# Three of four batches of x are turned by the host instead of TensorE, in an attention and mixture layer on one core

## The reference

```
x = x + layernorm(attention(layernorm(x)))
x = x + layernorm(ffn(layernorm(x)))
```

## Time and profile before

| | us |
|---|---|
| median of 3 runs | 1018.43 (1017.51 to 1020.02) |
| profiled execution | 1016.17 |
| its span, first to last instruction | 1014.4 |
| projection stage, within the span | about 0 to 297 |
| attention of the 32 groups | about 297 to 600 |
| output projection and ffn | about 600 to 1014 |

### The profile page before, as it was taken

The page is one execution under the profiler, slowest core; times in us unless marked ns, Lnnn a source line. Parts: engine busy times, 40 slices in busy tenths (PEclk is TensorE's granted clock), DMA queues, the critical chain, the costliest instruction groups (busy, mean ns, idle before and its releaser), DMA issues.

```text
span 1014.4 us, 17409 instructions
## 1 busy us (share of the span) xinstructions
PE 990.1 (98%) x6400; PEld 814.0 (80%) x6400; DVE 660.6 (65%) x1954; ACT 400.2 (39%) x682; POOL 455.2 (45%) x490
## 2 busy tenths in 40 slices
PE   6999999999999999999999999999999999999996
PEld 5888888898886666666666678999999999999996
DVE  7752443434558988998989666666666666666655
ACT  7331221210127777777777662222222222222211
POOL 1453542433439999999998911111111111111110
PEclk9999999999999999999999999999999999999998
DMA  9342442237247876765555463222222222222101
GB/s 354 151 146 84 146 145 84 83 116 195 99 148 197 217 197 173 186 163 151 140 140 145 138 209 99 86 83 84 83 83 84 84 84 83 83 79 77 54 22 41
DMA packets 78644, 127.23 MB, mean 125 GB/s; under 512 B 7776, under 2 KB 46944, under 8 KB 75488
## 3 DMA queue, kind: packets, MB, share of 16 engines
q1 hardware_dynamic: 78560, 126.13, 41.0%
HBM read 85.20 MB, written 40.37 MB: 124 GB/s over the span
## 4 chain that ended last, share of the span: by engine, by line
PE 92%; DVE 3%; DMA 2%; ACT 1%; POOL 1%; issue 1%; SPq 0%; POOLq 0%; DVEq 0%; ACTq 0%
PE bank L1287 21%; PE bank L1289 21%; PE bank L1288 21%; PE bank L1359 8%; PE bank L1381 7%; PE bank L1397 7%; DMA q_t<-shift_l 2%; PE bank L1421 2%; PE bank L1296 1%; PE bank L1547 1%; PE bank L1424 1%; PE bank L1427 1%; DVE wf_l L1195 1%; DVE bank L1018 1%; PE bank L1460 0%
## 5 line engine op out<-in xcount | busy, mean ns | idle before, releaser
L1018 DVE CUSTOM_DVE_ANT_0 bank<-bank,row_mask 128x384 f32<-128x384 f32 (+3 forms) x512 | 235.7, 517 | 49.9 <-PE bank L1359 49.8
L653 POOL TENSOR_TENSOR ln_rs<-ln_ve,minus_half 128x1 f32<-128x1 f32 x64 | 61.6, 962 | 392.6 <-DVE ln_mm L962 392.6
L837 ACT ACTIVATE prob<-bank 128x512 f32<-128x512 f32 x320 | 173.9, 599 | 34.8 <-PE bank L1381 34.5
L1287 PE MATMUL bank<-wf_h,xt_h 128*128 128x384 f32 (+1 forms) x384 | 129.7, 338 | 0.9 <-DVE z L1176 0.9
L1289 PE MATMUL bank<-wf_l,xt_h 128*128 128x384 f32 (+1 forms) x384 | 130.2, 339 | 0.0
L1288 PE MATMUL bank<-wf_h,xt_l 128*128 128x384 f32 (+1 forms) x384 | 129.6, 338 | 0.0
L1359 PE MATMUL bank<-k_t,q_t 96*128 96x384 f32 (+3 forms) x512 | 123.4, 337 | 0.4 <-DVE row_top L1018 0.3
L1287 PE MATMUL bank<-xt_h,wq_h 128*128 128x512 f32 x304 | 119.8, 394 | 0.0
L1289 PE MATMUL bank<-xt_l,wq_h 128*128 128x512 f32 x304 | 118.6, 390 | 0.0
L1288 PE MATMUL bank<-xt_h,wq_l 128*128 128x512 f32 x304 | 118.5, 390 | 0.0
L711 POOL TENSOR_TENSOR key_sum<-key_sum,prob 128x512 f32<-128x512 f32 x93 | 117.8, 1293 | 0.0
(11 more groups left out here) (118 smaller groups left out, 1882.4 us busy)
## 6 DMA issues: line engine op xcount, KB each, us to landing
q_t<-q_scratch SPq DMA_DIRECT2D x32, 512.0 KB, 5.5
q_scratch<-turn_h SPq DMA_DIRECT2D x16, 512.0 KB, 2.7
q_scratch<-turn SPq DMA_DIRECT2D x16, 512.0 KB, 3.0
q_t<-q_scratch SPq DMA_DIRECT2D x32, 256.0 KB, 5.8
att_scratch<-att SPq DMA_DIRECT2D x32, 256.0 KB, 2.5
at_raw<-att_scratch SPq DMA_DIRECT2D x16, 512.0 KB, 3.7
x<-x SPq DMA_DIRECT2D x16, 512.0 KB, 4.2
out<-z SPq DMA_DIRECT2D x15, 512.0 KB, 2.9
```

Source lines behind the costliest of these rows:

```text
L653: nc.gpsimd.tensor_tensor(ln_rs[j][:], ln_ve[j][:], minus_half[:], ALU.pow).then_inc(count, 1)
L837: nc.scalar.activation(prob[n % 2][:, i, :, :].rearrange("p h q -> p (h q)"), score_bank(n, i)[:], ACT.Exp, scale=INV_SQRT_HD).then_inc(pr ...
L1018: last = nc.vector.tensor_tensor_reduce(out=row, in0=row, in1=row_mask[:, SEQ - w:SEQ], scale=1.0, scalar=LOWEST, op0=ALU.add, op1=ALU.max ...
L1287: mm(dst, a_h, w_h, start=start, stop=False, skip_group_check=True)
```

## The change

The host hands over a second array, `x_t`: batches 1 to 3 of x, transposed, features on the partitions. The loads of x rows stay, with two row buffers instead of three, but serve only for the statistics. For batches 1 to 3:

- DVE's `stats1` writes minus the mean of each token, and POOL's `root` writes the root 1 / sqrt(var + eps), into a small tile `ln_pack` (128 tokens of a tile on the partitions, 2 numbers x 4 tiles).
- SP stores `ln_pack` to DRAM as two rows of 512 numbers (`store_stats`) and reads these back with every row copied to all 128 partitions, 512 KB (`load_stats`), into `token_stats`, which takes the place of the third row buffer.
- SP loads the raw transposed batch in four pieces of 512 KB (`load_turned`) into `xt_raw`, which lies where `xt_l` will be.
- DVE adds minus the mean and multiplies by the root in place (`normalise_turned`, two instructions of 128 x 1024 for each quarter g), ACT rounds to `xt_h` (`turned_to_hi`), and DVE subtracts (`turned_to_lo`, which turns `xt_raw` into `xt_l`).
- TensorE's `transpose1` is left for tiles 0 to 3 only. The first pair of batches 1 to 3 waits for the four quarters one after the other.

```diff
-XRING = 3
+XRING = 2
+TURNS = 4
+TURN = KC // TURNS
...
+    stat_scratch = nc.dram_tensor("stat_scratch", [BATCH - 1, 2, SEQ], F32).ap()
...
+            xt_raw.append(Map(m.at)(f"xt_raw{j}", [P, KC, SEQ]))
...
+        token_stats = m("token_stats", [P, 2, SEQ])
...
             def load_x(t):
+                wait(sp, ln1_step, 5 * (t - XRING) + 2 if t >= TT + XRING else 0)
                 r = (t - TT) % XRING
-                wait(sp, xt_ps, t - XRING + 1 if t >= TT + XRING else 0)
                 sp.dma_start(x_ring[r][:], x[t]).then_inc(x_loaded[r], 16)
+
+            def load_turned(b, g):
+                wait(sp, proj_ps, 2 * USES * (b - 1) if b >= 2 else 0)
+                chunks = slice(TURN * g, TURN * g + TURN)
+                sp.dma_start(xt_raw[b % 2][:, chunks, :], x_t[b - 1, :, chunks, :]
+                             ).then_inc(turned_loaded[g], 16)
+
+            def store_stats(b):
+                sp.wait_ge(ln1_step, 5 * TT * (b + 1))
+                sp.wait_ge(ln1_norm, 2 * TT + TT * b)
+                dst = stat_scratch[b - 1].rearrange("s (t p) -> p s t", p=P)
+                sp.dma_start(dst, ln_pack[b - 1][:], allow_slow_non_contiguous=True).then_inc(stats_stored, 16)
+
+            def load_stats(b):
+                sp.wait_ge(stats_stored, 16 * b)
+                wait(sp, turned_norm, TURNS * (b - 1))
+                sp.dma_start(token_stats[:], stat_scratch[b - 1].partition_broadcast(P)).then_inc(stats_loaded, 16)
...
-            for t in range(TT, TT + XRING):
+            for t in range(TT, 2 * TT):
                 load_x(t)
+            for g in range(TURNS):
+                load_turned(1, g)
...
-                    t = tile_after(b, p)
-                    if t is not None and t + XRING < NT:
-                        load_x(t + XRING)
+                    after, t = b + 1, TT * (b + 2)
+                    if after < BATCH and p == 0:
+                        store_stats(after)
+                        if b > 0:
+                            load_turned(after, 0)
+                            load_turned(after, 1)
+                        load_stats(after)
+                    if after < BATCH and b > 0 and p == 1:
+                        load_turned(after, 2)
+                        load_turned(after, 3)
+                    if t < NT and p == 1:
+                        load_x(t)
+                        load_x(t + 1)
+                    if t < NT and p == 3:
+                        load_x(t + 2)
                     if b == BATCH - 1 and p == 3:
                         load_shift(0)
                 for t in range(TT * b, TT * b + TT):
                     store_v(t)
+                if b + 2 < BATCH:
+                    load_x(TT * (b + 2) + 3)
...
+            def root(t):
+                pool.wait_ge(ln1_step, 5 * t + 5)
+                nc.gpsimd.tensor_tensor(ln_pack[t // TT - 1][:, 1, t % TT:t % TT + 1], ln_ve[t % LN][:],
+                                        minus_half[:], ALU.pow).then_inc(ln1_norm, 1)
+
+            root(TT)
+            root(TT + 1)
             for b in range(BATCH):
                 for p in range(PAIRS):
                     rope_pair(b, p)
-                    t = tile_after(b, p)
-                    if t is not None and t + 2 < NT:
-                        scale1(t + 2)
+                    if b + 1 < BATCH and p == 0:
+                        root(TT * (b + 1) + 2)
+                        root(TT * (b + 1) + 3)
+                    if b + 2 < BATCH and p == 2:
+                        root(TT * (b + 2))
+                if b + 2 < BATCH:
+                    root(TT * (b + 2) + 1)
...
+            def turned_to_hi(b, g):
+                if g == 0:
+                    act.wait_ge(xt_ps, TT)
+                    wait(act, proj_ps, 2 * USES * (b - 1))
+                act.wait_ge(turned_norm, TURNS * (b - 1) + g + 1)
+                chunks = slice(TURN * g, TURN * g + TURN)
+                nc.scalar.copy(xt_h[b % 2][:, chunks, :], xt_raw[b % 2][:, chunks, :]
+                               ).then_inc(turned_hi, 1)
...
-                    t = tile_after(b, p)
-                    if t is not None:
-                        ready_for(t)
+                    if b + 1 < BATCH and p >= 2:
+                        for g in ((0,), (1, 2), (3,))[p - 2]:
+                            turned_to_hi(b + 1, g)
...
-            def next_tile(t):
-                lo1(t)
-                if t + 2 < NT:
-                    stats1(t + 2)
+            def normalise_turned(b, g):
+
+                if g == 0:
+                    dve.wait_ge(stats_loaded, 16 * b)
+                dve.wait_ge(turned_loaded[g], 16 * b)
+                part = xt_raw[b % 2][:, TURN * g:TURN * g + TURN, :]
+                minus_mean, root = [token_stats[:, s, :].unsqueeze(1).broadcast_to([P, TURN, SEQ]) for s in range(2)]
+                nc.vector.tensor_tensor(part, part, minus_mean, ALU.add).then_inc(turned_centred, 1)
+                dve.wait_ge(turned_centred, TURNS * (b - 1) + g + 1)
+                nc.vector.tensor_tensor(part, part, root, ALU.mult).then_inc(turned_norm, 1)
+
+            def turned_to_lo(b, g):
+
+                dve.wait_ge(turned_hi, TURNS * (b - 1) + g + 1)
+                chunks = slice(TURN * g, TURN * g + TURN)
+                nc.vector.tensor_tensor(xt_l[b % 2][:, chunks, :], xt_raw[b % 2][:, chunks, :],
+                                        xt_h[b % 2][:, chunks, :].bitcast(F32), ALU.subtract
+                                        ).then_inc(turned_ready, 1)
 
             for b in range(BATCH - 1):
+                t = TT * (b + 1)
                 for p in range(PAIRS):
                     rope_half(b, p, 0)
                     rope_half(b, p, 1)
-                    t = tile_after(b, p)
-                    if t is not None:
-                        next_tile(t)
-                for t in range(TT * b, TT * b + TT):
-                    v_bias(t)
+                    if p == 0:
+                        stats1(t + 2)
+                        stats1(t + 3)
+                    elif p == 2:
+                        if t + TT < NT:
+                            stats1(t + TT)
+                        normalise_turned(b + 1, 0)
+                    elif p == 3:
+                        turned_to_lo(b + 1, 0)
+                        normalise_turned(b + 1, 1)
+                        normalise_turned(b + 1, 2)
+                    elif p == 4:
+                        turned_to_lo(b + 1, 1)
+                        turned_to_lo(b + 1, 2)
+                        normalise_turned(b + 1, 3)
+                v_bias(TT * b)
+                v_bias(TT * b + 1)
+                turned_to_lo(b + 1, 3)
+                v_bias(TT * b + 2)
+                v_bias(TT * b + 3)
+                if t + TT < NT:
+                    stats1(t + TT + 1)
...
             def project_pair(b, p):
 
                 u = USES * b + p
-                if p == 0:
-                    pe.wait_ge(xt_ready, TT * (b + 1))
                 wait(pe, evac, evacs(u - 2) if u >= 3 else 0)
                 for i in range(2):
                     for c in range(KC):
+                        if b > 0 and p == 0 and i == 0 and c % TURN == 0:
+                            pe.wait_ge(turned_ready, TURNS * (b - 1) + c // TURN + 1)
...
-            transpose1(TT)
             pe.wait_ge(wq_ready, 2 * KC)
             for p in range(2, PAIRS):
                 project_pair(0, p)
-                transpose1(TT + p - 1)
             for tt in range(TT):
                 project_v(0, tt)
             for b in range(1, BATCH - 1):
                 for p in range(PAIRS):
                     project_pair(b, p)
-                    if p < TT:
-                        transpose1(TT * (b + 1) + p)
                 for tt in range(TT):
                     project_v(b, tt)
             b = BATCH - 1
...
+        "x_t": np.ascontiguousarray(arr["L0_attn_x"][1:].transpose(0, 2, 1).reshape(BATCH - 1, KC, P, SEQ)
+                                    .transpose(0, 2, 1, 3)),```

How the instructions stand on the engines. First TensorE between the first and second pair of batch 1, before (`bank` is PSUM, `x_ring` a row buffer, `ident` the identity):

```order
L1287 MATMUL bank<-xt_h_83,wq_h 128x512
L1288 MATMUL bank<-xt_h_83,wq_l 128x512
L1289 MATMUL bank<-xt_l_84,wq_h 128x512
L1296 MATMUL bank<-ident,x_ring_90 128x128 [waits xt_ready,xn_ready]
L1296 MATMUL bank<-ident,x_ring_90 128x128 x7
L1287 MATMUL bank<-xt_h_83,wq_h 128x512 [waits evac]
L1288 MATMUL bank<-xt_h_83,wq_l 128x512
```

More of the change, by code:

```diff
@@ L166, in build @@
         ln_mm = [m(f"ln_mm{j}", [P, 1]) for j in range(LN)]
+        ln_pack = [m(f"ln_pack{j}", [P, 2, TT]) for j in range(BATCH - 1)]
         minus_half = m("minus_half", [P, 1])
@@ L294, in build @@
         xn_ready = sem("xn_ready")
+        stats_stored = sem("stats_stored")
+        stats_loaded = sem("stats_loaded")
```

(40 more changed lines are left out.)

32 lines of the change are left out of this document (11 added, 21 removed).

## The result

The changed kernel takes 1027.34 us in the median of 4 runs (1026.11 to 1028.30), the kernel before 1017.97 (1016.76 to 1020.02) on the same chip. The ratio is 1.0086, with a 95% interval of 1.0064 to 1.0108. The forecast was 1007.9, so the kernel is 9.4 us slower where I had said some 10 faster. The profiled execution took 1026.11 us.

A forecast was written before the change was run, and what follows sets the result against it. TensorE, busy 990.1 of 1014.4 us, was taken as the bound. From the median 1018.43, less 10.6 for transposes, with 0 for added waits, came 1007.8, forecast 1007.9 us; range 1005.5 to 1012.0.

The forecast's parts named there:

- The transposes: TensorE, projection: removing 12 groups of 8 at 0.88 us each saves 10.6 us, all reaching the end.
- Met waits cost nothing: TensorE, starts of batches 1 to 3: nine added waits, already met, cost 0, bounded at 0.9 us.
- a repeated row costs nothing: DVE's add and multiply with one row of 512 repeated take the ordinary 1.215 us.
- Rival 2: DVE reads a repeated row at half speed, 2.43 us, and alternates with POOL: 1030.6 us, chance 0.03.
- The statistics' way in batch 0: Through DRAM: store 7.6 us, landed at 52.3, copy at 57.2, tile 8 near 58.6; in time.
- Rival 3: Statistics late: from a 12.2 us store TensorE waits at batch 1's head; 1010.7 to 1029.7 us, chance 0.05.
- rival 1: DVE and POOL block each other; in batch 0 quarter 3 comes 5.6 us late: 1013.5 us, chance 0.12.
- the slack of 4.6: Batch 0's chain: last low part at 81.6, TensorE asks for quarter 3 at 86.2; 4.6 us to spare.
- a slack of 6.9: Batch 1's chain: last low part at 152.6, TensorE asks for quarter 3 at 159.5; 6.9 us to spare.
- Rival 4: Gain given back at the seam to the attention stage; if half were lost, 1013 us; chance 0.04.

The follow-up runs named there:

- e3: Changed kernel without statistics and normalisation of batches 1 to 3, raw x cast and split: 1009.32 us, ratio 0.992 to the kernel before.
- e1: Changed kernel with POOL's rope instructions in batches 0 to 2 on 8 columns instead of 512: 1009.11 us, ratio 0.9913 to the kernel before.
- e2: Changed kernel with `token_stats` filled once from other data, statistics neither stored nor read back: 1013.87 us, ratio 0.9962 to the kernel before.
- e4: Changed kernel with useless matmuls where TensorE idled (22, 9 and 15 in batches 1, 2, 3): 1020.36 us, ratio 1.0034 to the kernel before.
- e5: Changed kernel reordered: DVE's long work between evacuation halves, statistics one batch ahead, nothing left out: 1010.44 us, ratio 0.992 to the kernel before.

## Why the prediction was wrong

**The transposes: right.** 12 x 0.88 = 10.6; e3's projection ends 9.7 earlier, and the start to batch 1 shortened by 3.37 against 3.52.

**Met waits cost nothing, a repeated row costs nothing: right.** The additions and multiplications of `normalise_turned`, whose second operand is a repeated row, take 1.22 where POOL is idle. At the head of batch 3, where the low parts are in time, the pitch is 0.23 straight through. Rival 2's doubling did not come from there.

**The statistics' way in batch 0: late by 3.5 us.** I had the first quarter start at 60.4 (58.6 + 1.8); it starts at 63.91. SP's queue shows where:

```profile
44.88 0.36 SPq L438 DMA_DIRECT2D stat_scratch<-ln_pack  x1
53.59 0.33 SPq L443 DMA_DIRECT2D token_stats<-stat_scratch  x1
...
54.96 2.29 SPq L426 DMA_DIRECT2D x_ring<-x  x2
```

The store was issued when I said (44.7), and the read behind it 8.7 us later, not 7.6; tile 8, loaded beside that read of 512 KB, reached DVE at 62.22 and not at 58.6. (The copy of 4.4 us in the rows had gone into my sum as 4.9, without a reason; the read landed in 4.8 to 6.8.) The store of 1024 numbers, against which the Trainium skill has its rule in "DMA: Bandwidth & Descriptors", "Rules for kernel authors", took 8.7 to 10.8 us in this profile and up to 12.0 in e1. The rule's one descriptor for each element fits the page of the profile: 11136 packets under 512 B, against 7984 in e2, which has none of the three stores, some 1050 for each. The price took slack and, by the estimate at e1, no time by itself. Rival 3 had put the edge at a store of 12.2 us, and e1's of 12.0 left 0.05.

**The step that failed: rival 1's stretch.** I wrote that "at the stretch of the row, 1.65 / 1.215 = 1.36, nine instructions lose 9 x 0.435 = 3.9 us and nothing waits", and gave the whole rival 0.12. The nine lost 7.5 (the durations of the nine between 68.94 and 89.81 add up to 18.5, against 11.0), nearly twice the 3.9 and less than the 10.2 of a full turn. The row I scaled from was one multiplication that came in the middle of POOL's three sums. Its extra 0.44 us fits what was left of the sum then running, so it is a rest and not a factor that can be carried over; POOL lost 0.94 there, most of one DVE instruction. The bound from both sides had been written down, and I took the mild end. The Trainium skill had the right rule: "SBUF — State Buffer", section "Who interferes with whom", says that a DVE instruction with two SBUF inputs contends with a GpSimd instruction that reads SBUF, and that the port pair they share is an exclusive lock. The trace agrees, with 1.22 becoming 2.31 and 1.29 becoming 2.28.

Then the slack of 4.6: 3.5 of lateness and 7.5 of stretch make 11.0, 6.4 too much, and TensorE was idle for 5.3 at the seventh chunk and 0.3 at the fifth. I had weighed each danger against the whole slack by itself. The lateness alone would have passed, by e1; the stretch of 7.5 was above 4.6 by itself. That the wait of 5.3 is close to rival 1's 5.6 is luck: the rival had 10.2 of stretch and no lateness. In batches 1 and 2 I had a slack of 6.9 and let it swallow 5.1, one pair's rope. In batch 1 the nine lost 7.6, under two pairs, and DVE had idled 7.92 us before them (1.79 in e2) for a row tile that SP issued behind the read of the statistics. So both causes worked there too, and batch 2's head waited 2.07. That the kernel came out slower, near the 1030.6 of rival 2, came of another path than that rival's.

**Left out: what a wait costs besides itself.** Rival 1's price, 1013.5, was the wait alone. A wait of 5.11 us brought 2.9 more at 1.2 GHz, and the one of 3.37 in batch 3 about as much again. e4 gives back 5.2 us up to the end of the projection by busy-work, 7.0 in the medians.

**Left out: DVE's value tiles and SP's queue behind them.** Rival 4 said that the loads of the groups are "ordered on SP after the same events as before". The order was the same and the events were late: 5.9 us from head to first load, and 6.6 us lost in batch 3.

**Open.** The last 3.0 us, after the projection. 1.8 of it is a stretch from 560 to 590 at a granted clock of 0.94 instead of 1.00, behind a wait of 2 us for POOL's sums that all profiles have, before's too. The dip is in the profiles of e1, e2, e3 and e5 as well and not in those of before and e4, so it varies with the execution or with when the wait falls; I did not test which. Before's profiled execution is also 1.8 below the median of 1017.97, the changed kernel's 1.2 below. The other 1.2 us I cannot place. Less the dip's 1.7 to 1.8 where there is one, the stretch behind the projection lasts 717.2 (e1, e2) to 719.3 (e4) in the six profiles without the transposes, and 719.1 both in the changed kernel and in e5, which hardly waits. So this rest is no larger than the profiles differ among themselves, and nothing ties it to the waits.

## What to carry to other kernels

Before giving DVE work with two SBUF operands, lay its instructions beside POOL's on the timeline and let them run in turn in the sum; where POOL has gaps, put them there. Add up all that is late against one slack, and not each item against the whole of it. Where TensorE then still waits as long as it did here (5.11 and 3.37 us), price the half clock behind it, about 3 us each, and follow every other queue that stands behind the late engine.

## What the runs showed that I had not expected

- Two engines in turn cost both of them: 1.22 to 2.31 us on DVE and 1.29 to 2.28 on POOL for 1024 and 512 columns, and an instruction of DVE's caught at the rim of POOL's work takes something between (1.88).
- Idling of 5.11 and 3.37 us in the projection was followed by some 6 us at 0.50 of the clock; 2.07 us was not. A wait of 2 us in the attention stage was followed by a lower clock in five of the seven profiles.
- A store of 1024 single numbers holds the queue that waits for it for 8.7, 10.0 and 10.8 us in batches 0, 1 and 2, and for 12.0, 9.1 and 9.5 in e1; a copy of two rows to 128 partitions lands in 4.8 to 6.8.
